# The two gathers of a block's expert rows, issued four and eight weight chunks later

## What is computed

```python
x = x + L0(x)   # gates, sixteen causal decays of one gated signal, blended, projections, layernorm
x = x + L1(x)   # additive attention with a mask per sequence: softmax over 256 keys, pooled
# L2: 8 weighted experts and one shared expert, all dense, F = 1024
g = einsum('bsd,edf->ebsf', h, Wg);  u = einsum('bsd,edf->ebsf', h, Wu)
expert_outs = einsum('ebsf,efd->ebsd', silu(g) * u, Wd)
x = x + (1 - sg) * einsum('be,ebsd->bsd', gates, expert_outs) + sg * shared(h)
# L3, the "head": one shared MLP; its last 64 output columns come from an expert picked per sequence
h = gelu(x @ W1 + b1)                       # 256 -> 1024
shared_x = h @ W2 + b2                      # 1024 -> 192
We_sel = We[indices]                        # (16, 1024, 64): rows picked by the sequence's index
expert_x = einsum('bnh,bhp->bnp', h, We_sel) + be[indices]
x = x + concatenate([shared_x, expert_x], -1)
```

## Time and profile before

| | |
|---|---|
| median of 3 runs | 2878.59 us (2877.34 to 2883.39) |
| the profiled execution | 2876.17 us, span 2874.4 us |
| PE busy | 2818.4 us (98%) |
| DVE busy | 1846.4 us (64%) |
| ACT busy | 1390.2 us (48%) |
| POOL busy | 1233.3 us (43%) |
| PE clock granted, mean | 0.993 of full |
| DMA, mean | 70 GB/s |

### The profile page before, as it was taken

How to read it: one execution, slowest core, us unless ns; L and a number is a source line. 1 busy time by engine, 2 the same in 40 slices (tenths; PEclk the granted TensorE clock), 3 DMA queues, 4 the chain that set the end, 5 groups by cost and what they waited for, 6 DMA issues and landing times.

```text
span 2874.4 us, 36550 instructions
## 1 busy us (share of the span) xinstructions
PE 2818.4 (98%) x13018; PEld 2331.4 (81%) x13018; DVE 1846.4 (64%) x3017; ACT 1390.2 (48%) x2408; POOL 1233.3 (43%) x950
## 2 busy tenths in 40 slices
PE   8699999999999999999999999999999999999999
PEld 5488888788888888888788888888888888888888
DVE  8699778867777766556865666655776563333443
ACT  4544555465336633454534553344643473333445
POOL 5256434643463445433554345542455333333333
PEclk9899999999999999999999999999999999999999
DMA  4133332322112311111311131111221122111231
GB/s 150 60 116 99 90 94 78 111 92 93 57 48 68 115 48 50 48 50 48 94 45 48 56 92 45 48 45 52 74 70 57 47 87 63 50 45 44 72 92 57
DMA packets 85573, 201.22 MB, mean 70 GB/s; under 512 B 10312, under 2 KB 27152, under 8 KB 85392
## 3 DMA queue, kind: packets, MB, share of 16 engines
q1 hardware_dynamic: 82256, 190.38, 21.5%
q0 software_dynamic: 2560, 8.39, 1.0%
q10 hardware_dynamic: 576, 0.11, 0.0%
HBM read 190.75 MB, written 8.09 MB: 69 GB/s over the span
## 4 chain that ended last, share of the span: by engine, by line
PE 88%; DVE 7%; issue 2%; ACT 2%; DMA 1%; SPq 0%; DVEq 0%; ACTq 0%
PE bank L557 19%; PE bank L559 19%; PE bank L558 19%; PE ps_out L557 9%; PE ps_out L559 9%; PE ps_out L558 9%; DVE trace L1075 2%; DVE w_lo L1145 2%; DVE trace L1067 1%; PE bank L550 1%; PE bank L631 1%; DVE hid L1169 0%; DMA stat<-mod_rows 0%; ACT L867 0%; PE bank L679 0%
## 5 line engine op out<-in xcount | busy, mean ns | idle before, releaser
L1308 POOL TENSOR_TENSOR hid_lo<-hid,hid_hi 128x512 fp32r<-128x512 f32 x640 | 865.6, 1353 | 1581.2 <-ACT hid_hi L954 1580.9
L557 PE MATMUL bank<-res_lo,w_hi 128*128 128x512 f32 x2432 | 963.3, 396 | 6.2 <-DVE res_lo L1160 3.3
L559 PE MATMUL bank<-res_hi,w_hi 128*128 128x512 f32 x2432 | 953.1, 392 | 0.0
L558 PE MATMUL bank<-res_hi,w_lo 128*128 128x512 f32 x2432 | 951.9, 391 | 0.0
L1169 DVE TENSOR_TENSOR hid<-hid,bank 128x512 f32<-128x512 f32 x576 | 393.3, 683 | 540.8 <-PE bank L559 512.8
L926 ACT ACTIVATE hid<-bank 128x512 f32<-128x512 f32 x576 | 344.0, 597 | 663.9 <-PE bank L559 662.8
L1145 DVE TENSOR_TENSOR w_lo<-w_raw,w_hi 128x768 fp32r<-128x768 f32 (+2 forms) x520 | 513.5, 989 | 177.9 <-ACT w_hi L895 139.6
L895 ACT ACTIVATE w_hi<-w_raw 128x768 fp32r<-128x768 f32 x392 | 331.4, 845 | 540.0 <-PE ps_out L559 513.4
L559 PEld LDWEIGHTS bank<-res_hi,w_hi 128*128 128x128 f32 x2432 | 458.3, 188 | 103.3
L557 PEld LDWEIGHTS bank<-res_lo,w_hi 128*128 128x128 f32 x2432 | 458.8, 189 | 100.5 <-issue 6.7
L558 PEld LDWEIGHTS bank<-res_hi,w_lo 128*128 128x128 f32 x2432 | 459.3, 189 | 86.4
(11 more groups left out here) (179 smaller groups left out, 1624.4 us busy)
## 6 DMA issues: line engine op xcount, KB each, us to landing
w_raw<-in_chunks SPq DMA_DIRECT2D x392, 384.0 KB
w_raw<-in_head_chunks SPq DMA_DIRECT2D x64, 224.0 KB
x_in<-in_xT SPq DMA_DIRECT2D x16, 256.0 KB, 3.6
pre_x<-in_xT SPq DMA_DIRECT2D x14, 256.0 KB, 7.0
soma_rows<-pre_soma SPq DMA_DIRECT2D x14, 256.0 KB, 2.0
soma<-soma_rows SPq DMA_DIRECT2D x14, 256.0 KB, 3.1
out_yT<-acc SPq DMA_DIRECT2D x7, 512.0 KB, 2.8
acc<-in_sidew SPq DMA_DIRECT2D x2, 512.0 KB, 7.1
```

The lines of the kernel that those rows point to most:

```text
L557: mm(out, wh, xl, start=start and i == 0, stop=False, skip_group_check=not lone)
L558: mm(out, wl, xh, start=False, stop=False, skip_group_check=not lone)
L559: last = mm(out, wh, xh, start=False, stop=end, skip_group_check=not lone)
L1308: nc.gpsimd.tensor_tensor(hid_lo[i % DEPTH][:], hid[i % 3][:], f(hid_hi[i % DEPTH][:]), ALU.subtract).then_inc(s_hlo, 1)
```

## The change

The position of the two gathers in POOL's list moves. Before, lane s looked at chunk n - s of an item ("cut", n): lane 0 was issued at the cut of the last head chunk, lane 1 one chunk later. Now it looks at chunk n - 4(s + 1): lane 0 is issued four chunks later, lane 1 eight. The wait for `w_lo` of the last head chunk stays in front of each. Twelve gathers move (blocks 2 to 7, two lanes each). The lists of PE, DVE, ACT and SP are the same as before.

```diff
                     for s in range(BB):
-                        e, b, c = CHUNKS[x[1] - s] if x[1] >= s else CHUNKS[0]
-                        if e == HEAD and c == FC - 1 and b + 2 < NBLK:
+                        k = x[1] - 4 * (s + 1)
+                        e, b, c = CHUNKS[max(k, 0)]
+                        if k >= 0 and e == HEAD and c == FC - 1 and b + 2 < NBLK:
                             gather(b + 2, [s])
```

## The result

| | median | range, runs |
|---|---|---|
| before | 2876.75 us | 2873.42 to 2883.39, 16 |
| changed | 2884.68 us | 2879.26 to 2888.08, 16 |
| ratio, 95% interval | 1.0024 | 1.0017 to 1.0031 |

What follows compares the result with a forecast made beforehand. PE bounds the kernel, busy 2818.4 of 2874.4 us, so only its idle and half-clock time can return. -5.4 - 2.0 + 1.6 + 0.4 + 0.5 + 0.7 = -4.2 us, from 2878.6 to 2874.4 us; range 2867.5 to 2881.5.

Steps and rivals of the forecast that it cites:

- POOL's waits become zero, and no PE wait names POOL: Line 1284: POOL's 12.0 us of waiting for w_lo vanish; no listed PE wait is for POOL.
- The two long w_lo go, 7.4 us: Heads of blocks 0 and 2: w_lo of 9.71 and 8.44 us vanish, giving PE back 5.4 and 2.0 us.
- POOL's pile-up: Block 0's head: twelve POOL instructions piled up during the 4.17 us wait, then ran without pause and held DVE's w_lo.
- The w_lo at 1197.34: Expert stretch: a w_lo of 1.94 us got in after one POOL instruction, cited as agreeing with the contention rule.
- POOL's work in the old pause costs 1.6 + 0.4 + 0.5 = 2.5 us: Heads: POOL no longer rests while DVE finishes; 1.6 us in block 0, 0.4 in block 2, 0.5 in the other four.
- one and a half meetings: Block 0's head: w_lo beside POOL work, about 1.1 us per meeting; one and a half were taken as 1.6 us.
- the bound of 4.17 us: Block 0's head: the high end of the added cost, POOL winning each time and the whole pause handed on.
- Gathers at the new places, 0.7 us: Four and eight chunks later: each adds 0.96 to 1.50 us of POOL; PE's cost for all taken as 0.7 us.
- The rule: Shared SBUF ports: w_lo never waits longer than one POOL instruction; by it the sum would be 0 rather than -4.2 us.
- Slower: Heads: POOL keeps DVE off at every boundary, PE's acc wait grows from 1.83 to 6.0 us; +8.3 us, 2886.9; chance 0.10.
- Its condition: The slower case decides once the waits added for the acc, over all heads, pass the 7.4 us that can go.
- Nothing returned: Heads: long w_lo form again, POOL perhaps gapless without any wait; 2878.6 us, within 2877 to 2881; chance 0.25.

Runs made afterwards that it cites:

- waits alone: Kernel before with POOL's waits for w_lo kept at the old places and the twelve gathers left out: 2867.04 us, ratio 0.9967.
- the subtraction: Kernel before with each of the twelve gathers replaced, behind the old waits, by a POOL subtraction of the same tile: 2871.28 us, ratio 0.9982.

## Why the prediction was wrong, step by step

*POOL's waits become zero, and no PE wait names POOL.* Right, both.

*The two long w_lo go, 7.4 us.* This step failed. The w_lo of 9.71 and 8.44 us did go, and so did the 3.66 us behind the first. But w_lo of 7.15, 4.31 and 5.89 us took their place, in the same two heads, and PE waited 1.73, 1.78 and 1.86 us for what came behind them. With the new half-clock stretch at 1418.50, that is 7.1 of the 7.4 us back. The forecast took POOL's pile-up for their cause and so took the move for their cure. The runs with waits alone and with the subtraction show a pile-up without a long w_lo; what is needed is an indirect DMA at the head of a run. The trace of before had a hint: every w_lo of over 2.3 us in it began within a few instructions of a gather at line 1284. The w_lo at 1197.34 and the sum at 1198.42 took turns, with no gather near; the prediction cited them and did not ask what was different at 507.42.

*POOL's work in the old pause costs 1.6 + 0.4 + 0.5 = 2.5 us.* Right mechanism, too small. It measured 4.38 us in block 0, 1.34 in block 2, 0.75 and 0.71 in blocks 4 and 5, 7.2 us together. The sum counted one and a half meetings, at the price of a row of 1.72 us. The head's w_lo is four instructions, and each can lose a turn; in block 0 even the bound of 4.17 us was passed. This term was 4.7 us too small. With the 7.1 us that came back, -4.2 becomes +7.6 us, where 6.9 was measured.

*Gathers at the new places, 0.7 us.* They cost no more than at the old places, but both cost about 9 us (0.9999 against 0.9967 with the waits, 1.0024 against 0.9995 without).

*The rule.* The sentence of the prediction on the Trainium skill, page "SBUF — State Buffer", section "Who interferes with whom", said that by the rule the pile-up would not be the reason of the long w_lo. That was right. The sum of 0 that the same sentence gives was not worked out: without the gain of 7.4 us, the forecast's own costs (1.6, 0.4, 0.5 and 0.7) were left, +3.2 us. In the runs without an indirect DMA near a head no w_lo is longer than 2.08 us, one POOL instruction more than its own 0.8. The page states no exception to it; the trace has one, behind an indirect DMA.

*The rivals.* "Slower" came out, by the mechanism named: PE's wait for the acc of 1.83 us became 6.21 (6.0 was written), and next to nothing of the gain stayed. It had a chance of 0.10 and a price of +8.3 us; 6.9 was measured (7.9 in the medians). Its condition was put wrongly: POOL did not have to win every boundary, only one for each of DVE's small instructions, and the added acc waits (7.2 us) did not have to pass 7.4 us, because that gain did not come. That its price is near is in part luck: it let the gain stay away for another reason. "Nothing returned" was half right too: the long w_lo did form again, but not because POOL was too busy.

## What to carry to other kernels

A wait that costs nothing on the path can be worth keeping: here 12 us of idle time on POOL kept it away from a neighbour's short instructions just ahead of a result that PE waited for. Before such a wait is taken out, count the instructions of the other engine in that stretch that would alternate with its own; here each of four 64-column ones lost about 1.1 us, as much as a 448-column one does. And try an indirect DMA of POOL where POOL is about to wait anyway, rather than in front of a run of ready work: here that was worth 0.3%.

## What the hardware showed that was not expected

With an indirect DMA of 0.96 us at the head of a POOL run, DVE's w_lo of 0.8 us of work took 7.15, 8.44, 8.63 and 9.71 us, held until POOL's next pause; with an ordinary instruction of 1.04 to 1.82 us in its place, 2.08 us at most. Why an indirect DMA does this is not settled here: the runs show the trigger and what ends it, not what is held. Nor was another kind of DMA on POOL tried. The 16 mask gathers of line 1295 can't tell: in the trace of before each is followed by one POOL instruction at most before a pause, and a w_lo held for one turn looks the same with and without a gather. And two engines that alternate turn by turn were seen to slow each other by one instruction of the other per instruction of their own: 0.21 us became 1.3 us on DVE, 1.29 became 2.02 on POOL.
